# Vision tower kernel, opening of the schedule: order of the loads, of the image statistics and of the first convolutions

## What is computed

```python
concat = concatenate((x, left_up, right_up, left_down, right_down), axis=1)      # four shifts by 4 pixels
normed = (concat - mean) * rsqrt(var + 1e-7) * gamma + beta                      # mean, var per image
y = conv(normed, W, stride 8) + b                                                # 13 x 13 patches, E = 128
h = concatenate([cls_tok, y])                                                    # 170 tokens of 128
q, k, v = layernorm(h) @ Wq.T, @ Wk.T, @ Wv.T
for t in range(170):                                                             # tokens in order
    S = S + 0.01 * sum over the 64 images of outer(v[image, t], k[image, t])
    out[:, t] = S q[:, t]
h = h + out
h = h + ffn(layernorm(h))
```

## Time and profile before

| | |
|---|---|
| median of 3 runs | 243.22 us (242.46, 243.40, 243.22) |
| profiled execution | 244.94 us |
| its span in the trace | 243.1 us |
| granted TensorE clock, mean | 0.97 |
| busy: TensorE, weight load, VectorE, ScalarE, GpSimd | 217.7, 190.9, 142.0, 140.2, 164.0 us |
| DMA | 37.15 MB, mean 153 GB/s |

### The profile page before, as it was taken

One profiled execution on the slowest core, in us unless ns is written; L12 is line 12 of the kernel. 1 busy time (PEld: TensorE's weight loads), 2 busy tenths in 40 slices (PEclk: granted clock), 3 DMA queues, 4 the chain that ended last, 5 costly groups with the idle time before them and its releaser, 6 DMA issues.

```text
span 243.1 us, 4901 instructions
## 1 busy us (share of the span) xinstructions
PE 217.7 (90%) x1560; PEld 190.9 (79%) x1560; DVE 142.0 (58%) x594; ACT 140.2 (58%) x328; POOL 164.0 (67%) x142
## 2 busy tenths in 40 slices
PE   0399996998999999999999899999999999999660
PEld 0389894876889899888988788999988988977430
DVE  1749962453267477946588726627777534464462
ACT  6012101454536767767667758577667767798650
POOL 1058978899657799929999659629998531542221
PEclk9999999999999999999999999999999999999955
DMA  6999929726163237564372733432433343344344
GB/s 183 378 431 423 416 101 217 303 65 217 40 190 91 54 83 234 131 200 99 89 234 64 245 97 80 108 94 73 99 95 79 96 99 77 87 111 121 91 109 110
DMA packets 30143, 37.15 MB, mean 153 GB/s; under 512 B 4039, under 2 KB 26877, under 8 KB 29862
## 3 DMA queue, kind: packets, MB, share of 16 engines
q1 hardware_dynamic: 29708, 36.46, 50.3%
q10 hardware_dynamic: 410, 0.38, 0.4%
HBM read 19.77 MB, written 5.92 MB: 106 GB/s over the span
## 4 chain that ended last, share of the span: by engine, by line
PE 47%; POOL 21%; DMA 17%; DVE 7%; issue 4%; ACT 2%; SPq 0%; POOLq 0%; DVEq 0%; ACTq 0%
PE conv L434 17%; POOL scaled L345 13%; DMA rows<-x_windows 11%; PE vr_ps L473 7%; PE state_ps L480 7%; PE out L495 7%; DMA mixed<-values 6%; PE state_ps L483 5%; POOL g_low L891 3%; POOL ln_rstd L902 2%; POOL rho L897 2%; PE turn L465 2%; DVE scaled L345 2%; PE conv L440 1%; ACT state L605 1%
## 5 line engine op out<-in xcount | busy, mean ns | idle before, releaser
L434 PE MATMUL conv<-scaled,wt 128*128 128x256 f32 (+3 forms) x460 | 119.9, 370 | 10.0 <-DMA wt<-weight 10.0
L345 POOL TENSOR_TENSOR scaled<-rows,gam 128x832 f32<-128x832 f32 x60 | 94.0, 1583 | 3.3 <-PE conv L434 2.0
L434 PEld LDWEIGHTS conv<-scaled,wt 128*128 128x128 f32 x460 | 75.5, 194 | 13.5 <-DMA wt<-weight 10.0
L600 ACT ACTIVATE values<-vr_ps,rho 128x256 f32<-128x256 f32 x85 | 40.3, 474 | 33.0 <-PE vr_ps L473 30.7
L891 POOL TENSOR_TENSOR g_low<-g_t,g_high 128x512 fp32r<-128x512 f32 (+1 forms) x22 | 27.1, 1234 | 38.5 <-ACT g_high L587 38.5
L715 DVE SCALAR_TENSOR_TENSOR images<-out,rho,images 128x128 f32<-128x128 f32 (+1 forms) x85 | 28.4, 336 | 37.7 <-PE out L495 32.0
L605 ACT COPY state<-state_ps 128x256 f32<-128x256 f32 x85 | 31.7, 373 | 20.5 <-PE state_ps L483 18.8
L613 ACT ACTIVATE images<-images,ln_shift,ln_gain 128x128 f32<-128x128 f32 x81 | 36.9, 484 | 8.0 <-DVE ln_shift L747 8.0
L480 PE MATMUL state_ps<-mixed 128*128 128x128 f32 x170 | 36.6, 298 | 4.2 <-DMA mixed<-values 3.4
L480 PEld LDWEIGHTS state_ps<-mixed 128*128 128x128 f32 x170 | 29.3, 191 | 13.0 <-issue 6.7
L693 DVE BATCH_NORM_STATS2 ln_stats<-images 128x6 f32<-128x128 f32 x85 | 18.6, 280 | 31.7 <-ACT images L594 31.7
(11 more groups left out here) (106 smaller groups left out, 232.2 us busy)
## 6 DMA issues: line engine op xcount, KB each, us to landing
rows<-x_windows SPq DMA_DIRECT2D x13, 864.0 KB, 5.8
mixed<-values SPq DMA_DIRECT2D x170, 64.0 KB, 2.0
out<-images SPq DMA_DIRECT2D x42, 128.0 KB, 2.4
images<-x_rows SPq DMA_DIRECT2D x3, 624.0 KB, 21.7
images<-x_rows SPq DMA_DIRECT2D x1, 1456.0 KB, 13.0
images<-x_rows SPq DMA_DIRECT2D x1, 1248.0 KB, 15.5
images<-x_rows SPq DMA_DIRECT2D x1, 832.0 KB, 19.6
small<-smalls SPq DMA_DIRECT2D x1, 512.0 KB, 8.6
```

The source lines that it names most:

```text
L345: return eng.tensor_tensor(scaled[:, s, at:at + N], window, gains, ALU.mult)
L434: last = pe.matmul(conv_ps[g % 2][:, at:at + n * B], wt[:, s], scaled[:, s, a % RING:a % RING + n], start=first, stop=(g < EARLY and s == ...
L600: act.activation(values[:, t % VALUE_SLOTS].rearrange("p a e -> p (a e)"), vr_ps[:, 0:2 * E], ACT.Identity, scale=rho[:, t + 1:t + 2]).the ...
```

## The change

- **Loads.** Weights second, row 1 before `small`, the image in seven parts of 16, 16, 20, 16, 16, 8 and 12 pixel rows (before: six of 28, 24, 12, 16, 12, 12); row 2 follows the third part, row 3 (still after VectorE's scaling of row 0) the fifth.
- **TensorE.** 16 float32 matmuls of zeros (128 x 128) ahead of everything; shifts 0 and 1 of group 1 before the tables; group 3 whole and shifts 0 and 1 of group 4 before the image sums; shift 2 of group 4, new in the opening (`EARLY_SHIFTS` 3), after them. Two items fewer are left for the steps.
- **GpSimd.** Row 1 first, the power for the class token after it; the powers of the image variance after three shifts of row 3 instead of two.
- **VectorE.** The low parts of the tables after the fourth image part instead of the second.
- **ScalarE.** Group 3 is copied out before the scale columns.

```diff
+WARM = 16
+
-EARLY_SHIFTS = 2
+EARLY_SHIFTS = 3
-STAT_CHUNKS = [(0, 28), (28, 24), (52, 12), (64, 16), (80, 12), (92, 12)]
+STAT_CHUNKS = [(0, 16), (16, 16), (32, 20), (52, 16), (68, 16), (84, 8), (92, 12)]
...
             sp.dma_start(gam[:], gamma).then_inc(gamma_in, 16)
+            sp.dma_start(wt[:], weight).then_inc(weight_in, 16)
             load_row(0)
             sp.dma_start(rows[:, ROW_SLOTS - 1, N:2 * N + 1], first_offsets).then_inc(first_offsets_in, 16)
-            sp.dma_start(wt[:], weight).then_inc(weight_in, 16)
+            load_row(1)
             sp.dma_start(small[:], smalls).then_inc(small_in, 16)
-            load_row(1)
+            load_images(0)
             sp.dma_start(bet[:], beta).then_inc(beta_in, 16)
-            load_images(0)
             load_images(1)
+            load_images(2)
             load_row(2)
-            for i in range(2, len(STAT_CHUNKS)):
-                load_images(i)
+            load_images(3)
+            load_images(4)
             sp.wait_ge(scaled_first, SHIFTS)
             load_row(3)
+            load_images(5)
+            load_images(6)
...
+            pe.wait_ge(zeros_ready, 1)
+            for _ in range(WARM):
+                pe.matmul(out_ps[0][:, 0:E], zeros[:], zeros[:], start=True, stop=True, skip_group_check=True)
...
+            conv_shifts(1, 0, 2)
             pe.wait_ge(gamma_in, 16)
...
-            conv_shifts(1, 0, SHIFTS)
+            conv_shifts(1, 2, SHIFTS)
...
-            conv_shifts(3, 0, 3)
+            conv_shifts(3, 0, SHIFTS)
+            conv_shifts(EARLY - 1, 0, 2)
             pe.wait_ge(sums_ready, 2)
...
-            conv_shifts(3, 3, SHIFTS)
+            conv_shifts(EARLY - 1, 2, EARLY_SHIFTS)
...
-            conv_shifts(EARLY - 1, 0, EARLY_SHIFTS)
...
             group_out(2)
+            group_out(3)
             act.wait_ge(image_power_ready, 1)
...
-            group_out(3)
...
-                if i == 1:
+                if i == 3:
                     for blk, ps in enumerate((turn_ps, terms_ps)):
...
-            pool.wait_ge(consts_ready, 2)
-            pool.wait_ge(ln1_var_ready, 1)
-            pool.tensor_tensor(rho[:, 0:1], ln1_var[:, 0:1], powers[:, 0:1], ALU.pow).then_inc(rho_ready, 1)
...
-                    if r == EARLY_ROWS - 1 and s == 2:
+                    if r == 2 and s == 0:
+                        pool.wait_ge(consts_ready, 2)
+                        pool.wait_ge(ln1_var_ready, 1)
+                        pool.tensor_tensor(rho[:, 0:1], ln1_var[:, 0:1], powers[:, 0:1], ALU.pow).then_inc(rho_ready, 1)
+                    if r == EARLY_ROWS - 1 and s == 3:
```

## The result

| | before | changed |
|---|---|---|
| median | 243.3 us (4 runs) | 248.64 us (4 runs: 247.94, 250.70, 249.35, 247.61) |
| ratio to before | | 1.0238, interval 1.0163 to 1.0313 |
| profiled execution, its span | 244.94, 243.1 us | 247.94, 246.1 us |
| first product of terms | 41.50 | 45.21 |
| first to last `g_low` | 43.43 to 221.12: 177.7 | 47.17 to 225.80: 178.6 |

The kernel became 5.3 us slower; I had forecast 3.1. The profiled executions lie only 3.0 us apart, since that of before had a long end: the clock fell at 230 there, and the end took 1.7 us more than in the changed kernel. What stands in front of the end is 3.71 us in the opening and 0.9 us in the steps.

The account below looks back on a forecast made before the run. TensorE, busy 217.7 of 243.1 us, was the bound, with parked tables setting its first product of terms. 1.2 + 1.9 - 0.9 + 0.9 = +3.1 us on the 243.22 median gave 246.3 us; range 243.0 to 248.0.

Parts of the forecast that it names:

- the two terms that made the 3.1: First product of terms 1.2 us later through the parked tables, and 1.9 us for a falling TensorE clock.
- The loads: Opening: last image part at 33.4 instead of 30.9, sums at 36.7, own scales at 40.9, still ahead of the terms.
- GpSimd's early start: Opening: row 1 starts near 12.1 instead of 15.24; the 3 us won go into the wait for the image variance.
- The sums' matmul: Opening: TensorE through with group 3 and two shifts of group 4 by some 35; sums ready at 36.7.
- The terms, +1.2: Opening: parked DMAs go at 27.0, 1.7 us later; first product of terms at 42.7, 1.2 us later.
- The bound of 1.7: Upper end for the parked tables' delay: they keep their 10.1 us from issue to landing.
- the end of the parked tables: After the loads, one engine drains the rest at 20 GB/s; the 41 rows of the second parked DMA run on one.
- The clock, +1.9: TensorE's clock falls to 1.2 GHz before the steps, delaying the chain to `rho` by 1.9 us; chance 0.50.
- the gap at 35 to 43: TensorE has about 2 us of work in the 7.7 us from 35 to 42.7, so its clock falls.
- The 3.5 us of my upper bound: Clock fall's upper price: all TensorE work at half speed as long as at the start, 3.5 us from 10.
- The steps, -0.9 + 0.9: Steps: two items fewer save 0.9 us; row loads asked for a step earlier, ahead of `mixed` copies, cost 0.9.
- The zeros, 0: Opening: the 16 matmuls of zeros are over before row 0 is scaled; nothing waits for them, so 0.

Follow-up runs that it names:

- Experiment 5: Changed kernel with the small weights' centering, centering matrix and class token copy moved from VectorE to ScalarE: 245.94 us, ratio 1.0109 to the kernel before.
- experiment 6: Kernel before with only the third shift of group 4 in the opening (`EARLY_SHIFTS = 3`) and its effect on the steps' plan: 245.97 us, ratio 1.0079.
- experiments 1: Changed kernel with only GpSimd's early start undone, the class token's power first again: 246.96 us, ratio 1.0108 to the kernel before.
- 12: Changed kernel without the 16 products of zeros: 251.75 us, ratio 1.0311 to the kernel before.
- 15: Changed kernel without the 16 products of zeros, measured a second time: 250.56 us, ratio 1.0268 to the kernel before.
- experiments 2: Changed kernel with the image sums' matmul ahead of group 3's last shift and group 4's three shifts: 248.89 us, ratio 1.0187 to the kernel before.
- 13: Changed kernel unaltered, measured once more, giving its second profiled execution: 249.81 us, ratio 1.0257 to the kernel before.
- 14: Changed kernel with three and four products of zeros filling the gaps ahead of the first product of terms: 249.08 us, ratio 1.0234 to the kernel before.
- experiment 10: Kernel before with parked DMA cut into 32 and 9, group 4's third shift early with old scaling steps, its shift 0 before scale columns' wait: 242.77 us, ratio 0.9955.

## Why the forecast was wrong

**Direction right, size too small:** 3.1 us forecast, 5.3 measured, above the range's 248.0. That the direction came out right is in good part luck: of the two terms that made the 3.1, neither is what held the first product. Term by term:

- *The loads* (last image part 2.5 us later, sums 36.7, no gain for GpSimd): confirmed as such. Alone they put the sums at 37.3 and cost 0.8 us. In the changed kernel the sums came at 38.10: VectorE was behind by then and ran its statistics from 32.05 on without waiting for any part.
- *GpSimd's early start, costed at nothing:* this is **the step that failed**. I wrote that the 3 us it wins go into a wait, and looked only at what GpSimd waits for, not at what VectorE does beside it. It holds four VectorE operations for 4.8 us more than before, with TensorE's small products behind them, and for 1.4 us the last scaling of row 0 ahead of them. Experiment 5 puts the price of the four at 2.9 us. The trace of before could have told: `ln_gain` took 0.17 us in one group of steps and 1.54 in another, beside a scaling (experiment 6).
- *The sums' matmul:* I had TensorE through with group 4's two shifts by 35, idle. It was behind by the lost time, and the sums waited 3.3 us for it. I never asked what is queued ahead of the sums if TensorE comes late.
- *The terms, +1.2:* the fetch was 3.1 us later, but own scales decided. The bound of 1.7 assumed VectorE on time. That the end of the parked tables is slow by its shape was right and worth a repair.
- *The clock, +1.9:* wrong place. In the changed kernel the gap at 35 to 43 existed in the forecast only. The clock does fall, in some executions, behind the wait for the held operations, and the first product is then 1.7 to 2.6 us later (46.90, 47.09, 47.78); behind the first product it fell in three traces (experiments 1, 12 and 15). I take this for the better part of what lies between the 4.6 us of opening and steps and the measured 5.3, and of the scatter of 3 us, but no run shows that share: with the early gap filled the ratio was still 1.0213, 5.2 us. I had priced a certain fall; it is one that comes or not. The 3.5 us of my upper bound stand in no row either: the lower level lasted to 14.87 in the trace of the kernel before, 4.9 us from the first convolution matmul.
- *The steps, -0.9 + 0.9:* the sum was 0, the traces show +1.0 for the plan (178.7 against 177.7; the runs of experiment 6 lose 1.9) and 0 for the items. The row loads that I priced cost nothing by step 40; the loss is the held pair at steps 53 to 55.
- *The zeros, 0:* right, within the 0.4% that experiments 12 and 15 leave open.

3.7 (opening) and 0.9 (steps) of the 5.3 are read from a trace. The other 0.7 is not shown term by term; a clock that falls in some executions is my estimate for it, and what experiment 6 loses beyond its trace is another candidate. How often the clock falls is not settled. Of the six traces in which GpSimd held VectorE and the gap behind group 0 was left open, four have the lower level behind it (experiments 2, 13, 14 and 15) and two don't (the first, and 12). Executions without a trace give only their mean clock, in which the start and the end weigh too: in experiment 15 it goes with the time (249.2 us at 0.988 twice, 251.9 at 0.970), in 13 it says little (248.1, 249.6 and 250.7 us, all at 0.976).

## What to carry to other kernels

Before an engine's work is moved earlier, look at what VectorE or GpSimd runs beside it then: an operation can be held for the other's whole instruction, and a four-column operation waits as long as a big one. Price a move by who stands behind the held instruction, in each engine's own order. A schedule that is derived from a count (here, the items left for the steps) moves everything behind it; keep the old places of what is tuned. A store whose slow end shows as a DMA share of one engine in sixteen is worth cutting another way, as the one of 41 partitions here.

## What the runs showed of the hardware that I had not expected

- A VectorE operation of 0.17 to 0.28 us took 1.2 to 1.6 beside GpSimd's scaling of 1.58, and one of 1.02 us took 2.40, while `bn_stats` and `bn_aggr` kept their time.
- A store of 41 partitions delayed its landing by 1.6 us against 32 and 9.
- The clock fell in some executions of one program and not in others: between 20 and 27 us it was 1.00 in the first trace of the changed kernel and 0.76 in the second, with TensorE busy all the time. Ahead of it, from 17.4 to 19.8, TensorE had worked 0.34 us and none; its whole wait was 2.18 and 3.49 us.
- Experiment 12, without a fall in its opening, had one 1.1 us behind the start of the first product, and experiment 10 one at 139.2, behind 1.85 us of work in 3.90.
